# Output projection with the weights stationary, its bias on ScalarE, its result turned back by TensorE

## The reference

```python
xn = group_norm(x)                                   # 32 groups per image
qkv = xn @ qkv_w.T + qkv_b                           # with two low-rank terms of rank 4 on q and v
attn = softmax(scale * q @ k.T + rel_h + rel_w)      # 196 x 196 per head
out = attn @ v                                       # back to (tokens, 768)
return x + (out @ proj_w.T + proj_b)
```

## Time and profile before

| | us |
|---|---|
| median of 3 runs | 3608.06 |
| the runs | 3602.63 to 3608.63 |
| the profiled execution | 3603.43 |
| its span, first to last instruction | 3601.9 |
| PE busy | 3447.5 |
| DVE busy | 2573.5 |
| ACT busy | 2019.3 |
| POOL busy | 35.7 |
| mean granted TensorE clock | 0.985 |

### The profile page before, as it was taken

The page is one execution under the profiler, slowest core; times in us unless marked ns, Lnnn a source line. Parts: engine busy times, 40 slices in busy tenths (PEclk is TensorE's granted clock), DMA queues, the critical chain, the costliest instruction groups (busy, mean ns, idle before and its releaser), DMA issues.

```text
span 3601.9 us, 81066 instructions
## 1 busy us (share of the span) xinstructions
PE 3447.5 (96%) x32612; PEld 2313.4 (64%) x32612; DVE 2573.5 (71%) x6042; ACT 2019.3 (56%) x5459; POOL 35.7 (1%) x65
## 2 busy tenths in 40 slices
PE   5789999999999999999999999999999999999997
PEld 3556666666666666666666666666666666666665
DVE  5677777777777777777777777777777777777764
ACT  1466555555555555555656555556555555655553
POOL 0000000000000000000000000000000000000000
PEclk9899999999999999999999999999999999999998
DMA  4145555555455545455555565555455554555444
GB/s 120 35 98 108 111 107 110 104 107 111 102 104 112 106 102 114 100 107 107 109 105 111 97 116 102 106 105 109 102 115 104 108 104 104 104 115 105 108 94 92
DMA packets 992579, 376.18 MB, mean 104 GB/s; under 512 B 922307, under 2 KB 972483, under 8 KB 992206
## 3 DMA queue, kind: packets, MB, share of 16 engines
q1 hardware_dynamic: 976366, 333.63, 47.3%
q10 hardware_dynamic: 15840, 37.38, 3.6%
HBM read 86.61 MB, written 38.54 MB: 35 GB/s over the span
## 4 chain that ended last, share of the span: by engine, by line
PE 75%; DVE 14%; ACT 5%; DMA 1%; issue 1%; SPq 1%; POOL 0%; POOLq 0%; DVEq 0%; ACTq 0%
PE ring L614 39%; PE ring L684 20%; PE score L657 7%; PE o_ps L671 5%; ACT prob L740 3%; DVE split L854 3%; PE ring L692 2%; PE ring L681 2%; DVE rel_sb L823 2%; DVE row_max L831 2%; DVE q_lo L798 1%; DVE xT L802 1%; DVE rel_sb L817 1%; DVE split L845 1%; DMA rel_q<-rel_sb 1%
## 5 line engine op out<-in xcount | busy, mean ns | idle before, releaser
L614 PE MATMUL ring<-xn_hi,w_hi 128*128 128x392 f16 x3456 | 1149.9, 333 | 62.4 <-DVE rel_sb L823 57.7
L614 PE MATMUL ring<-xn_hi,w_lo 128*128 128x392 f16 x3456 | 1147.5, 332 | 0.0
L614 PE MATMUL ring<-xn_lo,w_hi 128*128 128x392 f16 x3456 | 1147.5, 332 | 0.0
L740 ACT ACTIVATE prob<-score,neg_max,exp_scale 98x196 f32<-98x196 f32 x1536 | 770.3, 511 | 484.2 <-DVE neg_max L835 476.5
L854 DVE SCALAR_TENSOR_TENSOR split<-prob,row_inv,split 98x196 f16<-98x196 f32 x1536 | 544.6, 418 | 12.4
L614 PEld LDWEIGHTS ring<-xn_hi,w_hi 128*128 128x128 f16 x3456 | 340.4, 98 | 317.3 <-DVE rel_sb L823 64.8
L684 PE MATMUL ring<-w_hi,o_hi 128*98 128x384 f16 x1536 | 501.7, 327 | 0.0
L684 PE MATMUL ring<-w_hi,o_lo 128*98 128x384 f16 x1536 | 501.7, 327 | 0.0
L684 PE MATMUL ring<-w_lo,o_hi 128*98 128x384 f16 x1536 | 501.5, 327 | 0.0
L614 PEld LDWEIGHTS ring<-xn_hi,w_lo 128*128 128x128 f16 x3456 | 340.8, 99 | 240.7 <-issue 8.8
L614 PEld LDWEIGHTS ring<-xn_lo,w_hi 128*128 128x128 f16 x3456 | 341.0, 99 | 224.2 <-issue 8.6
(11 more groups left out here) (121 smaller groups left out, 4919.8 us busy)
## 6 DMA issues: line engine op xcount, KB each, us to landing
y_sb<-in_x SPq DMA_DIRECT2D x256, 147.0 KB
out<-y_sb SPq DMA_DIRECT2D x256, 147.0 KB
x_sb<-in_x ACTq DMA_DIRECT2D x31, 1176.0 KB
rel_q<-rel_sb SPq DMA_DIRECT2D x128, 147.0 KB, 3.0
stage<-in_L_conv_qkv_w SPq DMA_DIRECT2D x3, 2304.0 KB, 18.9
turned<-split SPq DMA_TRANSPOSE x384, 4.0
v_tok<-v_split SPq DMA_TRANSPOSE x192, 3.4
stage<-in_L_conv_proj_w SPq DMA_DIRECT2D x1, 2304.0 KB, 20.1
```

Source lines behind the costliest of these rows:

```text
L614: last = T.matmul(ring[:, bank, 0:NT], w[:, c, 128 * j:128 * j + 128], xx[:, t.par, c, :], start=(c == 0 and part == 0), stop=(c == CT - 1 ...
L740: last = A.activation(prob[:, step[3], head, half, :], score[0:HALF, head, TOK * half:TOK * half + TOK], ACT.Exp, bias=neg_max[:, step[3], ...
```

## The change

Y becomes six steps, one for each 128 output channels. The weights are stationary and the 392 tokens move, so the result has channels on partitions. ACT copies it to `yT` (two buffers) with `proj_b` as its per-partition bias and `y_scale` as its scale. A new step Z follows on PE, behind the next Y step or other work: four fp32 transposes of `yT` with 98 tokens each into one ring bank, 98 x 512, and DVE adds that to x in `y_sb`. `y_sb` has three slots of 98 x 4 x 128, so loads and stores go in pieces of 128 channels. The bias rows and their preparation go. All four orders are written anew. Cut to its core:

```diff
@@ -38,8 +37,7 @@
-YC = C // 2
-YS = 8
+YS = 3
...
@@ -66,17 +64,17 @@
 MIDDLE = (
     [unit("P", 1, 10)] + each("V", 0, 0) + each("R", 0, 4) + [unit("P", 1, 11)] + each("K", 0, 1)
     + each("Y", 1, 0) + each("X", -1, 0, 1, 2, 3, 4, 5)
-    + score(0) + each("Y", 1, 1) + each("V", 0, 1)
-    + score(1) + each("Y", 1, 2) + each("K", 0, 2) + each("G", -1, 0)
-    + score(2) + each("Y", 1, 3) + each("V", 0, 2) + each("G", -1, 1)
-    + score(3) + each("Y", 1, 4) + each("K", 0, 3)
-    + score(4) + each("Y", 1, 5) + each("V", 0, 3)
-    + score(5) + each("Y", 1, 6) + each("K", 0, 4)
-    + score(6) + each("Y", 1, 7) + each("V", 0, 4)
-    + score(7) + each("Q", -1, 0) + each("K", 0, 5)
-    + score(8) + each("Q", -1, 1) + each("V", 0, 5)
-    + score(9) + each("Q", -1, 2) + each("Q", -1, 3)
-    + score(10) + each("Q", -1, 4, 5)
+    + score(0) + each("Y", 1, 1) + each("Z", 1, 0) + each("V", 0, 1)
+    + score(1) + each("Y", 1, 2) + each("Z", 1, 1) + each("G", -1, 0)
+    + score(2) + each("K", 0, 2) + each("G", -1, 1) + each("Y", 1, 3) + each("Z", 1, 2)
+    + score(3) + each("V", 0, 2) + each("Y", 1, 4) + each("Z", 1, 3)
+    + score(4) + each("K", 0, 3) + each("Y", 1, 5) + each("Z", 1, 4)
+    + score(5) + each("V", 0, 3) + each("Z", 1, 5) + each("Q", -1, 0)
+    + score(6) + each("K", 0, 4) + each("Q", -1, 1)
+    + score(7) + each("V", 0, 4) + each("Q", -1, 2)
+    + score(8) + each("K", 0, 5) + each("Q", -1, 3)
+    + score(9) + each("V", 0, 5) + each("Q", -1, 4)
+    + score(10) + each("Q", -1, 5)
     + score(11) + each("K", -1, 0) + each("R", -1, 0, 1, 2, 3))
 
 
@@ -90,37 +88,35 @@
 
 ACT_ORDER = (
     each("LD", -1, 0) + each("V", 0, 0) + each("R", 0, 4) + [unit("P", 1, 11)] + each("K", 0, 1)
...
+    + each("Y", 1, 0) + each("X", -1, 0, 1, 2, 3, 4, 5)
+    + soft(0) + each("Y", 1, 1) + each("V", 0, 1)
+    + soft(1) + each("Y", 1, 2)
+    + soft(2) + each("H", -1, 0) + each("K", 0, 2) + each("Y", 1, 3)
+    + out_of(1) + soft(3) + each("H", -1, 1) + each("V", 0, 2) + each("Y", 1, 4)
+    + soft(4) + each("H", -1, 2) + each("K", 0, 3) + each("Y", 1, 5)
+    + out_of(3) + soft(5) + each("V", 0, 3) + each("Q", -1, 0)
+    + soft(6) + each("K", 0, 4) + each("Q", -1, 1)
+    + out_of(5) + soft(7) + each("V", 0, 4) + each("Q", -1, 2)
+    + soft(8) + each("K", 0, 5) + each("Q", -1, 3)
+    + out_of(7) + soft(9) + each("V", 0, 5) + each("Q", -1, 4)
+    + soft(10) + each("Q", -1, 5)
     + out_of(9) + soft(11) + each("K", -1, 0) + each("R", -1, 0, 1, 2, 3))
 
 
 DVE_ORDER = (
...
+    each("V", 0, 0) + [unit("P", 1, 11)] + each("R", 0, 4) + each("K", 0, 1)
     + each("X", -1, 0, 1, 2, 3) + [unit("S", 0, 0)] + each("X", -1, 4, 5) + [unit("N", 0, 0)] + each("M", -1, 0)
...
+    + [unit("T", 0, 0)] + each("Z", 1, 0)
+    + [unit("S", 0, 1)] + each("V", 0, 1) + soft(1) + each("Z", 1, 1) + each("G", -1, 0)
+    + [unit("S", 0, 2)] + each("G", -1, 1) + soft(2) + each("H", -1, 0) + each("K", 0, 2) + each("Z", 1, 2)
+    + [unit("S", 0, 3)] + out_of(1) + each("H", -1, 1) + soft(3) + each("V", 0, 2) + each("L", -1, 0) + each("Z", 1, 3)
+    + [unit("S", 0, 4)] + each("H", -1, 2) + soft(4) + each("K", 0, 3) + each("L", -1, 1) + each("Z", 1, 4)
+    + [unit("S", 0, 5)] + out_of(3) + each("L", -1, 2) + soft(5) + each("V", 0, 3) + each("Z", 1, 5) + each("Q", -1, 0)
+    + [unit("S", 0, 6)] + soft(6) + each("K", 0, 4) + each("Q", -1, 1)
+    + [unit("S", 0, 7)] + out_of(5) + soft(7) + each("V", 0, 4) + each("Q", -1, 2)
+    + [unit("S", 0, 8)] + soft(8) + each("K", 0, 5) + each("Q", -1, 3)
+    + [unit("S", 0, 9)] + out_of(7) + soft(9) + each("V", 0, 5) + each("Q", -1, 4)
+    + [unit("S", 0, 10)] + soft(10) + each("Q", -1, 5)
     + [unit("S", 0, 11)] + out_of(9) + soft(11) + each("K", -1, 0) + each("R", -1, 0, 1, 2, 3))
 
 
@@ -128,19 +124,18 @@
 
 
 SP_ORDER = (
-    each("VT", 0, 0) + each("CR", 0, 0) + each("ST", 1, 0)
-    + [unit("T", 0, 0)] + each("ST", 1, 1)
-    + each("VT", 0, 1) + [unit("T", 0, 1)] + each("ST", 1, 2) + each("LY", 1, 4)
-    + [unit("T", 0, 2)] + each("ST", 1, 3) + each("LY", 1, 5)
-    + each("VT", 0, 2) + [unit("T", 0, 3)] + each("ST", 1, 4) + each("LY", 1, 6)
-    + [unit("T", 0, 4)] + each("ST", 1, 5) + each("LY", 1, 7)
-    + each("VT", 0, 3) + [unit("T", 0, 5)] + each("ST", 1, 6)
-    + [unit("T", 0, 6)] + each("ST", 1, 7)
-    + each("VT", 0, 4) + [unit("T", 0, 7), unit("T", 0, 8)] + each("LY", 0, 0, 1, 2, 3)
-    + each("VT", 0, 5) + [unit("T", 0, u) for u in range(9, 12)])
-RING_KINDS = ("Q", "K", "V", "R", "Y", "X", "G")
+    each("VT", 0, 0) + each("CR", 0, 0)
+    + [unit("T", 0, 0)] + each("ST", 1, 0)
+    + each("VT", 0, 1) + [unit("T", 0, 1)] + each("ST", 1, 1) + each("LY", 1, 3)
+    + [unit("T", 0, 2)] + each("ST", 1, 2) + each("LY", 1, 4)
+    + [unit("T", 0, 3)] + each("VT", 0, 2) + each("ST", 1, 3) + each("LY", 1, 5)
+    + [unit("T", 0, 4)] + each("ST", 1, 4)
+    + [unit("T", 0, 5)] + each("VT", 0, 3) + each("ST", 1, 5)
+    + [unit("T", 0, 6), unit("T", 0, 7)] + each("VT", 0, 4) + each("LY", 0, 0, 1, 2)
+    + [unit("T", 0, 8), unit("T", 0, 9)] + each("VT", 0, 5) + [unit("T", 0, 10), unit("T", 0, 11)])
+RING_KINDS = ("Q", "K", "V", "R", "Y", "Z", "X", "G")
 RING_STEPS = [s for s in MIDDLE if s[0] in RING_KINDS]
-PER_PAIR = {"Q": 6, "K": 6, "V": 6, "R": RCH, "Y": YS, "X": 6, "G": 2}
+PER_PAIR = {"Q": 6, "K": 6, "V": 6, "R": RCH, "Y": 6, "Z": 6, "X": 6, "G": 2}
...
@@ -581,17 +556,15 @@
                                                split[:, image].rearrange("r a b c d k -> r (a b c d k)")
                                                ).then_inc(turned_in[image], 16)
                     elif kind == "ST":
-                        wait(sp, read["Y"], YS, t.q, k + 1)
-                        sp.dma_start(out_rows[t.q][:, k // 2, YC * (k % 2):YC * (k % 2) + YC],
-                                     y_sb[:, k % 4]).then_inc(y_out[k % 4], 16)
+                        wait(sp, read["Z"], 6, t.q, k + 1)
+                        sp.dma_start(out_rows[t.q][:, :, 128 * k:128 * k + 128], y_sb[:, k % YS]).then_inc(y_out[k % YS], 16)
                     elif kind == "LY":
-                        if not (phase == "first" and k < 4):
-                            wait(sp, y_out[k % 4], 32, t.q, 16 * (k // 4))
-                        sp.dma_start(y_sb[:, k % 4], x_rows[t.q][:, k // 2, YC * (k % 2):YC * (k % 2) + YC]
-                                     ).then_inc(y_in[k % 4], 16)
+                        if not (phase == "first" and k < YS):
+                            wait(sp, y_out[k % YS], 32, t.q, 16 * (k // YS))
+                        sp.dma_start(y_sb[:, k % YS], x_rows[t.q][:, :, 128 * k:128 * k + 128]).then_inc(y_in[k % YS], 16)
 
             walk(sp, steps, SP_ORDER, pairs - 2)
-            for slot in range(4):
+            for slot in range(YS):
                 sp.wait_ge(y_out[slot], 16 * 2 * pairs)
 
         @block.tensor
@@ -675,14 +648,18 @@
                     elif kind == "Y":
                         if k == 0:
                             wait(pe, o_lo_made, 6, t.q, 6)
-                        tok = slice(HALF * (k // 2), HALF * (k // 2) + HALF)
-                        to = ring[0:HALF, bank, 0:YC]
-                        out_c = slice(YC * (k % 2), YC * (k % 2) + YC)
-                        T.matmul(to, ones[:, :], bias_rows[:, out_c], start=True, stop=False)
+                        j = 3 * CT + k
                         for c in range(HP):
                             for part, (w, oo) in enumerate(((w_hi, o_hi), (w_hi, o_lo), (w_lo, o_hi))):
-                                last = T.matmul(to, oo[:, o_slot(t.par, c), tok], w[:, c, 3 * C:][:, out_c],
-                                                start=False, stop=(c == HP - 1 and part == 2))
+                                last = T.matmul(ring[:, bank, 0:NT], w[:, c, 128 * j:128 * j + 128],
+                                                oo[:, o_slot(t.par, c), :],
+                                                start=(c == 0 and part == 0), stop=(c == HP - 1 and part == 2))
+                        last.then_inc(done[kind], 1)
+                    elif kind == "Z":
+                        wait(pe, read["Y"], 6, t.q, k + 1)
+                        for i in range(4):
+                            last = T.transpose(ring[0:HALF, bank, 128 * i:128 * i + 128],
+                                               yT[:, k % 2, HALF * i:HALF * i + HALF], ident[:, :])
                         last.then_inc(done[kind], 1)
                     elif kind == "X":
                         if k == 0:
@@ -756,6 +733,11 @@
                         wait(act, pv_done, 12, t.q, 2 * k + 2)
                         A.activation(o_hi[:, o_slot(t.par, k), :], o_ps[:, 0:NT], ACT.Identity,
                                      bias=bias[:, 2 * CT + k:2 * CT + k + 1]).then_inc(o_hi_made, 1)
+                    elif kind == "Y":
+                        wait(act, done[kind], 6, t.q, k + 1)
```

(47 more changed lines are left out.)

5 lines of the change are left out of this document (removed).

## The result

The changed kernel takes 3622.36 us (median of 6 runs, 3619.78 to 3625.43) against 3607.64 us for the kernel before (median of 6, 3602.38 to 3609.05, on the same chip). The ratio is 1.0044, 95% interval 1.0031 to 1.0057: slower by 0.4%. I had forecast 3608, no change. The profiled execution took 3625.43 us, with a span of 3623.7.

What follows compares the result with a forecast made beforehand. PE was taken to bound each pair up to unit 10's scores, a VectorE chain from there to V step 0; -6 + 14 - 5.5 - 3.4 + 1 = 0 gave 3608 us, range 3576 to 3642.

Steps and rivals of the forecast that it cites:

- TensorE's sum: PE's work per pair: 24.9 us of Y removed, 17.9 of new Y and 3.0 of Z added, net 4.0 less.
- The first part: V step 0 to unit 10's scores, set by PE: 88.58 - 4.0 + 2.99 = 87.6 us per pair.
- The ring count and the second part: Unit 10's scores to next V step 0: 43 ring steps, not 39, so wait for R step 1; 18.8 us.
- a pair without low clock: First and second part summed: 106.4 us against 106.57, 0.2 us less per pair, 6 us over 30 pairs.
- The clock: Slow V step 0 after the longer pause, every pair: 1.3 us, 0.45 more than now, +14 us; bounds -8 and +26.
- Outside the pairs: Preparation -5.5 us without the bias rows, last output -3.4, first and last pair +1.
- the case's own range: Forecast's case, chance 0.55: 3590 to 3626 us, from the bounds of the clock and Z.
- VectorE's chain in slots 1 to 9: Rival, between unit 1's and unit 10's `row_max`: VectorE's chain exceeds PE's 68.0 us, total 3623 to 3653; chance 0.22.
- Transposes overlap: Against the rival that Z's transposes each cost their whole 0.30 us, 4.2 us per pair, total 3738; chance 0.03.
- The cheap pause: Rival at V step 0: longer pause takes most of the slow stretch, clock -8, Z -9: 3577 us; chance 0.15.
- The full relief: Rival: PE's 4.0 us per pair count in full, V step 0 not waiting for the later R step: 3477; chance 0.05.

Runs made afterwards that it cites:

- pause filled: Changed kernel with 24 matmuls of 392 columns, result unused, on PE ahead of V step 0: 3556.59 us, ratio 0.9873 to the kernel before.
- the kernel before with its pause filled: Kernel before with 10 unused matmuls of 392 columns ahead of V step 0: 3582.42 us, ratio 0.9945 to the kernel before.
- two unused ring places: Changed kernel with two unused places in the ring's count before K step 0, so V step 0 takes K step 0's bank: 3496.65 us, ratio 0.9708.

## Why the prediction missed

Its parts were the length of V step 0 to unit 10's scores, that of the chain behind it, the clock, and what lies outside the pairs.

- **TensorE's sum.** Predicted -4.0 per pair, measured -4.1 in busy time at full clock. A Z step costs 0.53 us to the next work, where 0.50 stood. The Trainium skill, TensorE: Matmul & The Clock Gate, Part 4, has about 275 ns for a bf16 transpose in one kernel; that is its duration in fp32 here too, 273 ns, but in a row they start 0.11 us apart, and the sum has to go by that.
- **The first part.** Predicted 87.6 us. Measured 88.53 in a pair with 1.3 of low clock, so 87.2.
- **The ring count and the second part.** Predicted 18.8 us, a wait for R step 1, and 1.2 at unit 11's scores. Measured 18.75, R step 1, and 1.19. The waits come to 132.8 and 38 more where 140 and 37 stood.
- **So a pair without low clock** is 106.04 us (pause filled) against 106.57: 0.5 less where I had 0.2 less. Against the mean pair of the kernel before with its pause filled, 106.72, it is 0.7 less.
- **The clock is the step that failed.** "I take it in every pair" was right. "I take 1.3" per pair was not: it is 2.1 (108.15 - 106.04). It was mis-sized, and the bound of 1.7 was passed too. I had taken the slow stretch of the earlier trace rows (4.67 for 2.99, so 1.68) as the largest there is and let a part of it fall in the pause. But that row, at 0.63, is itself a mixture of the two levels. A V step 0 wholly at 1.2 GHz takes nearly twice 2.99 (5.85 and 5.86 are the longest in these runs), so 2.9 is the bound, and one pair in three comes near it: 2.7, 1.3 and 2.3 us are lost in turn. The pairs show the same: 108.75, 107.28 and 108.23 against 106.01 with the pause filled. Over 30 pairs that is (2.1 - 0.83) x 30 = +38 us where +14 stood and +26 was the bound. The term for the kernel before was off as well: 12 of 30 V steps 0 are slow, not half, and the filled pause gives 0.68 per pair, so 0.15 of the 0.83 are other waits. Told that way the clock is +43 and the pair without it -20; the sum is the same.
- **Outside the pairs.** The preparation gives what was said: x is first turned at 103.5 us (pause filled) instead of 108.6, 5.1 less for 5.5. The end gains more than 3.4: from the last pair's first transpose of x to the end it is 221.4 us against 228.5, 7.1 less. The first pair loses more than 1: from its first scores to the third pair's transposes it is 101.5 against 94.3, of which 1.6 is clock (99.9 with the pause filled). The two nearly cancel, as forecast (-3.4 and +1), but each is some 6 to 7 us.

Summed with the measured terms: -0.5 x 30 + 38 - 5.1 - 7.1 + 5.6 = +16 us, against 14.7 between the medians. The profiled execution is 22 above, of which its later load makes 4.7. The clock alone would have put me off by 24 us; that the miss is only 14 is luck, as the shorter pair without low clock gives 9 of them back. Two figures of the prediction don't follow from its rows: 0.53 scaled by 128/98 is 0.70 and not 0.72, and the case's own range, 3590 to 3626, is narrower than its bounds: the clock's alone give 3586 to 3620, Z's 3599 to 3647.

Of the rivals, VectorE's chain in slots 1 to 9 did not become the bound: apart from unit 11's, waits for exponentials are as before. Where it comes nearest is slot 3: unit 3's maximum starts 4.14 us after its scores (1802.22 above), the exponentials end 3.4 after that, and the slot is 7.94 long, a margin of 0.4.

```profile
1806.36 0.96 DVE L813 TENSOR_REDUCE row_max<-score 98x4 f32<-98x784 f32 x1
```

By unit 9 VectorE has caught up to 2.28, so the chain did not hold back the relief of TensorE ahead of unit 10's scores: it counted in full there. Transposes overlap. The cheap pause was wrong in sign. The full relief was rightly excluded as the kernel stands, and two unused ring places bring most of it: 3496.65, where 3477 stood.
